# One written list of steps for the change of phases in a graph layer, with the key contexts back to back on TensorE

## The reference, cut to what matters

```python
xn = _layernorm(x)
# graph part: out[dst] += (xn @ weight[rel])[src] * norm
transformed = jnp.einsum('ni,rio->rno', xn, weight)          # 16 types
gnn = segment_sum(transformed[rel_type, src] * norm, dst, num_segments=N)
# mix part: softmax of the keys over the nodes, context of each head, gate
k = softmax(k, axis=1); context = einsum('bnhd,bnhv->bhdv', k, v)
mix = einsum('bnhd,bhdv->bnhv', q, context) * sigmoid(gelu(...) @ Wg2 + bg2) @ Wproj + bproj
x = x + gnn + mix
# experts on the layer norm of the new x, top 2 of 8
tokens = _layernorm(x); out = tokens
for e in range(8):
    out = out + combine[:, e:e+1] * (gelu(tokens @ w1[e] + b1[e]) @ w2[e] + b2[e])
x = x + out
```

## Time and profile before

| | us |
|---|---|
| median of 3 runs | 1601.22 |
| lowest and highest run | 1599.69, 1601.41 |
| span of the profiled execution | 1685.8 |
| its TensorE busy, share of the span | 1601.8, 95% |

### The profile page before, as it was taken

One profiled execution on the slowest core, in us unless ns is written; L12 is line 12 of the kernel. 1 busy time (PEld: TensorE's weight loads), 2 busy tenths in 40 slices (PEclk: granted clock), 3 DMA queues, 4 the chain that ended last, 5 costly groups with the idle time before them and its releaser, 6 DMA issues.

```text
span 1685.8 us, 31748 instructions
## 1 busy us (share of the span) xinstructions
PE 1601.8 (95%) x10509; PEld 1451.7 (86%) x10509; DVE 1340.2 (79%) x3389; ACT 961.4 (57%) x2156; POOL 999.6 (59%) x1111
## 2 busy tenths in 40 slices
PE   7999999999999989998789999999999999999998
PEld 6888888777877878786689999999999999999998
DVE  7888565577777777775569999889999999999985
...
GB/s 295 267 258 246 235 226 238 222 242 242 259 249 242 257 228 252 238 265 271 203 98 100 108 104 112 100 102 101 117 101 106 101 116 100 99 109 110 104 62 10
DMA packets 127076, 290.50 MB, mean 172 GB/s; under 512 B 21271, under 2 KB 49724, under 8 KB 126914
## 3 DMA queue, kind: packets, MB, share of 16 engines
...
## 4 chain that ended last, share of the span: by engine, by line
PE 67%; DVE 12%; issue 8%; ACT 6%; another core or an unknown queue 3%; POOL 2%; DMA 1%; SPq 0%; DVEq 0%; ACTq 0%; POOLq 0%
PE bank L1821 52%; PE bank L2025 3%; PE bank L2026 2%; PE bank L1865 2%; PE bank L1866 2%; ACT mh L1030 2%; DVE ml L1606 2%; DVE ml_a L1357 1%; POOL stg L814 1%; PE bank L1977 1%; DVE ht L1722 1%; DVE xres L1736 1%; ACT raw L1086 1%; DVE stg L1224 1%
## 5 line engine op out<-in xcount | busy, mean ns | idle before, releaser
L814 POOL DMA_INDIRECT stg<-table,idxcur x495 | 530.6, 1072 | 263.9 <-issue 172.9
L1821 PE MATMUL bank<-wreg,xt 128*128 128x512 f32 x2352 | 589.9, 401 | 7.3 <-issue 6.5
L1821 PEld LDWEIGHTS bank<-wreg,xt 128*128 128x128 f32 x2352 | 438.6, 191 | 100.5 <-issue 11.4
L696 POOL DMA_INDIRECT raw<-table,idxa x297 | 302.5, 1018 | 147.3 <-issue 85.4
L1821 PE MATMUL bank<-tt,wreg 128*128 128x256 f32 (+1 forms) x2400 | 319.5, 282 | 0.0
L1821 PE MATMUL bank<-wreg,ht 128*128 128x256 f32 x2352 | 314.7, 283 | 0.4 <-DVE ht L1722 0.2
L1821 PEld LDWEIGHTS bank<-tt,wreg 128*128 128x128 f32 x2400 | 296.4, 189 | 2.9
L1821 PEld LDWEIGHTS bank<-wreg,ht 128*128 128x128 f32 x2352 | 293.2, 189 | 0.9 <-DVE ht L1722 0.4
L1086 ACT ACTIVATE raw<-bank,cols 128x256 f32<-128x256 f32 (+1 forms) x400 | 164.4, 462 | 132.7 <-remote 72.6
L1224 DVE COPY stg<-bank 128x512 f32<-128x512 f32 x196 | 134.2, 686 | 110.4 <-PE bank L1821 76.1
L1606 DVE SCALAR_TENSOR_TENSOR ml<-stg,nrm,mh 128x256 fp32r<-128x256 f32 x455 | 195.5, 478 | 13.4 <-ACT mh L1030 12.8
...
## 6 DMA issues: line engine op xcount, KB each, us to landing
...
```

The source lines that it names most:

```text
L696: pool.indirect_dma_start(ring_a[:, r * EARLY + j, :], None, table[0:LIMIT, :], bass.IndirectOffsetOnAxis(ap=idxa[:, at:at + 1], axis=0)). ...
L814: pool.indirect_dma_start(stg[:, (s % 4) * SUP + j, :], None, table, bass.IndirectOffsetOnAxis(ap=idxcur[:, at:at + 1], axis=0)).then_inc( ...
L1821: mm = pe.matmul(dst, stat(a, c), mov(b, c), start=(n == 0), stop=(n == 3 * chunks - 1))
```

## The change

The first twenty-four groups of sums (pairs 0, 1 and 2), pair 0's way through the experts, and pair 1's up to its second expert are no longer taken from slot tables. One list, `CHANGE`, names their steps in order; `follow` runs it on every engine, which takes the entries that it has a step for. The slot table takes over at pair 3. `SLOTS_OF_SECOND`, `PARTS_OF_SLOT`, `SPLITS` and the lines that hung steps on slots go. In detail:

- On TensorE the held rows and all six parts of the returned rows stand back to back, and pair 0's first sums behind them. The contexts' further steps stand between pair 0's sums.
- The shifts and exponentials of parts 0 and 1 stand ahead of the end of phase one on VectorE and ScalarE. SP issues the loads of the first five rows behind the second table store of the last tile, the other two of `slot` when the kept contexts are done.
- Pair 0's experts begin behind group 3 of pair 1, not behind group 7, with the sums of pair 1 and of pair 2 between them.
- The splits of expert weights are in halves of a chunk, eight on each engine, spread over the list.
- Whole f32 messages are used for the first 20 groups, not the first 16.
- `hf` and the small tiles of the expert choice move out of `raw`, to `ctxbd` with `dg`, to `wv`, and to a new tile `mix`.
- The activation table for Gelu is loaded in pair 0's sums. `roots2` for pair 0 goes ahead of the second gather of group 4 of pair 1 (now: the first of group 5), for pair 1 ahead of group 5 of pair 2 (now: the second of group 7).

```diff
-    ROOTS, FIRST_ROOTS = (7, 1), (5, 0)
+    ROOTS, EARLIER_ROOTS = (7, 1), {1: (4, 1), 2: (5, 0)}
+    FREE_ROWS = 5
...
-        hf = [rs[:, 2048 + 512 * b:2560 + 512 * b] for b in range(2)]
+        hf = [cd[:], wv[:].rearrange("p c n -> p (c n)")]
...
+                    if at(k, NT - 1) and h == 1:
+                        sp.wait_ge(sum_a, ER)
+                        for b2 in range(2):
+                            sp.wait_ge(kv_st[b2], 16 * ((KEPT + SLOTS) // 2))
+                        for n in range(FREE_ROWS):
+                            load_row(n // 4, n)
...
-            load_rows(0)
-            load_rows(1)
+            sp.wait_ge(ctx1_mm, KEPT)
+            for n in range(FREE_ROWS, SLOTS):
+                load_row(1, n)
             first_phase_over(sp)
...
+            def SPLIT(n, h):
+                act.wait_ge(raw_in[n % 2], 32 * (n // 2 - 1))
+                if n >= 6:
                     act.wait_ge(ctx_mm, HELD + REST)
+                act.copy(wreg[:, HI, place_of(n), h * CC // 2].rearrange("p r o -> p (r o)"),
+                         raw[:, n % 2, h * WC * C:(h + 1) * WC * C]).then_inc(w_hi, 1)
...
-WHOLE = 2
+WHOLE_GROUPS = 20
...
+CHANGE = (
+    "HELD_ROWS", "ROWS_OF 0", "FADE", "SELECT 0 0", "SELECT 0 1", "ROWS_OF 1", "SHIFT 2", "EXP 2", "ROWS_OF 2", "SHIFT 3",
+    "EXP 3", "ROWS_OF 3", "MSGS 0 0", "SHIFT 4", "EXP 4", "ROWS_OF 4", "MSGS 0 1", "SHIFT 5", "EXP 5", "ROWS_OF 5", "MSGS 0 2",
+    "GELU_TABLE", "MSGS 0 3", "SPLIT 4 0",
+    "CONTEXT", "SUMS 0 0", "CONTEXT_PE", "SUMS 0 1", "SELECT 0 2", "CONTEXT_TURN", "VALUES", "SUMS 0 2", "ADDS 0 0",
+    "SELECT 0 3", "HEADS", "QUERY", "SUMS 0 3", "CLEAR", "SELECT 0 4", "MSGS 0 4", "QUERY_ROWS", "GATES 0 2", "GATE_ACT 0 2",
+    "SUMS 0 4", "OUT 0 2", "ADDS 0 1", "SPLIT 4 1", "SELECT 0 5", "GATE 0 2", "GATE_HI 0 2", "MSGS 0 5", "SUMS 0 5",
+    "GATE_LOW 0 2", "PROJ 0 2", "ADDS 0 2", "SELECT 0 6", "MSGS 0 6", "SUMS 0 6", "SPLIT 5 0", "SELECT 0 7", "MSGS 0 7",
+    "SUMS 0 7", "SPLIT 5 1", "SELECT 1 0", "MSGS 1 0", "SUMS 1 0", "ADDS 0 3", "SELECT 1 1", "MSGS 1 1", "SUMS 1 1", "ADDS 1 0",
+    "STATS 0 2", "SELECT 1 2", "MSGS 1 2", "SUMS 1 2", "SPLIT 6 0", "MEAN 0 2", "NORM 0 2", "SPLIT 6 1", "TURN 0 2",
+    "TURN_HI 0 2", "TURN_LOW 0 2", "MSGS 1 3", "SELECT 1 3", "LAYER1 0 2 0", "LOGIT 0 2", "SUMS 1 3", "LAYER1 0 2 1",
+    "TOP 0 2", "LOW 0 2 0", "ADDS 1 1",
+    "WEIGHT 0 2", "SELECT 1 4", "LOW 0 2 1", "SPLIT 7 0", "COMB 0 2", "COMB_HI 0 2", "MSGS 1 4", "LAYER1 0 2 2",
+    "LAYER2 0 2 0", "OUT 1 2", "SUMS 1 4", "GATES 1 2",
+    "COMB_LOW 0 2", "SELECT 1 5", "ADD 0 2 0", "LOW 0 2 2", "GATE_ACT 1 2", "GATE 1 2", "LAYER1 0 2 3", "LAYER2 0 2 1",
+    "GATE_HI 1 2", "MSGS 1 5", "SUMS 1 5", "SPLIT 7 1",
+    "ADD 0 2 1", "SELECT 1 6", "LOW 0 2 3", "GATE_LOW 1 2", "ADDS 1 2", "LAYER1 0 2 4", "LAYER2 0 2 2", "MSGS 1 6",
+    "SUMS 1 6", "COMBT 0 2",
+    "ADD 0 2 2", "SELECT 1 7", "LOW 0 2 4", "COMBT_ACT 0 2", "LAYER1 0 2 5", "PROJ 1 2", "LAYER2 0 2 3", "MSGS 1 7",
+    "SUMS 1 7",
+    "ADD 0 2 3", "SELECT 2 0", "LOW 0 2 5", "ADDS 1 3", "LAYER1 0 2 6", "MSGS 2 0", "LAYER2 0 2 4", "SUMS 2 0",
+    "SELECT 2 1", "MSGS 2 1", "SUMS 2 1",
+    "ADD 0 2 4", "LOW 0 2 6", "ADDS 2 0", "STATS 1 2", "SELECT 2 2", "LAYER1 0 2 7", "MSGS 2 2", "LAYER2 0 2 5", "SUMS 2 2",
+    "BIAS2 0 2", "SELECT 2 3",
+    "ADD 0 2 5", "MEAN 1 2", "NORM 1 2", "LOW 0 2 7", "BIAS2_ADD 0 2", "MSGS 2 3", "LAYER2 0 2 6", "SUMS 2 3", "TURN 1 2",
+    "TURN_HI 1 2", "TURN_LOW 1 2", "ADDS 2 1", "SELECT 2 4", "MSGS 2 4", "SUMS 2 4", "SELECT 2 5",
+    "ADD 0 2 6", "LAYER1 1 2 0", "LOGIT 1 2", "MSGS 2 5", "LAYER2 0 2 7", "LOW 1 2 0", "SUMS 2 5", "LAYER1 1 2 1", "TOP 1 2",
+    "ADD 0 2 7", "ADDS 2 2", "SELECT 2 6", "MSGS 2 6", "SUMS 2 6", "SELECT 2 7", "MSGS 2 7", "SUMS 2 7",
 )
+def follow(order, **steps):
+    for entry in order:
+        name, *numbers = entry.split()
+        if name in steps:
+            steps[name](*map(int, numbers), *((8,) if name in OF_GROUPS else ()))
...
-    for i in range(2, pairs):
+    for i in range(3, pairs):
```

More of the change, by code:

```diff
@@ L1010, in _ @@
             held_exps()
+            for ready in range(2):
+                EXP(ready)
             first_phase_over(act)
@@ L1022, in MSGS @@
                 at = EB * (4 * i + s // 2) + EARLY + (s % 2) * CUT
-                if isinstance(i, int) and i < WHOLE:
+                if whole(S):
                     for j in range(n):
@@ L1093, in slot_of @@
             def slot_of(i, s, groups, p1, n1, p2, n2):
-                if s == 0 and not isinstance(i, int):
-                    act.activation(small[0:1, 156:157], small[0:1, 157:158], ACT.Gelu).then_inc(table_kept, 1)
-                if isinstance(i, int) and i + s == 0:
-                    beside(i, s)
                 in_slot(i, s, groups, p1, n1, p2, n2, MSGS=MSGS, GATE_ACT=GATE_ACT, GATE_HI=GATE_HI, NORM=NORM,
                         TURN_HI=TURN_HI, WEIGHT=WEIGHT, COMB_HI=COMB_HI, COMBT_ACT=COMBT_ACT, LAYER1=LAYER1)
-                if isinstance(i, int) and (i, s) == (0, 7):
-                    query_high()
-                    GATE_ACT(0, 2)
-                if isinstance(i, int) and i + s > 0:
-                    beside(i, s)
+            follow(CHANGE, EXP=EXP, SPLIT=SPLIT, GELU_TABLE=GELU_TABLE, QUERY_ROWS=QUERY_ROWS, MSGS=MSGS,
+                   GATE_ACT=GATE_ACT, GATE_HI=GATE_HI, NORM=NORM, TURN_HI=TURN_HI, WEIGHT=WEIGHT, COMB_HI=COMB_HI,
+                   COMBT_ACT=COMBT_ACT, LAYER1=LAYER1)
             run(slot_of, NP, TAIL_GROUPS)
@@ L1598, in MSGS @@
                     return
-                if isinstance(i, int) and i < WHOLE:
+                S = 8 * i + s
+                if whole(S):
                     return
                 at = EB * (4 * i + s // 2) + EARLY + (s % 2) * CUT
-                done = (EB - EARLY) * (4 * i + s // 2) + (s % 2) * CUT
+                done = tiles_before(S)
                 for j in range(PART[s % 2]):
@@ L1766, in slot_of @@
             def slot_of(i, s, groups, p1, n1, p2, n2):
-                if isinstance(i, int) and i + s == 0:
-                    for part in PARTS_OF_SLOT[0]:
-                        shifts(part)
-                    fade_kept()
                 in_slot(i, s, groups, p1, n1, p2, n2, SELECT=SELECT, MSGS=MSGS, WINDOW=WINDOW, LAST_WINDOW=LAST_WINDOW, GATE=GATE,
@@ L1970, in held_contexts, with ROWS_OF @@
                     mm.then_inc(ctx_mm, 1)
-            def contexts(part):
+            def ROWS_OF(part):
                 rows = rows_of(part)
@@ L2151, in _ @@
             pe.wait_ge(add_a, ALL_ADDS)
+            follow(CHANGE, HELD_ROWS=HELD_ROWS, ROWS_OF=ROWS_OF, CONTEXT_PE=CONTEXT_PE, VALUES=VALUES, QUERY=QUERY,
+                   SUMS=SUMS, OUT=OUT, GATES=GATES, PROJ=PROJ, TURN=TURN, LOGIT=LOGIT, COMBT=COMBT, BIAS2=BIAS2,
+                   LAYER1=LAYER1, LAYER2=LAYER2)
             run(slot_of, NP, TAIL_GROUPS)
@@ L2181 @@
 )
-SLOTS_OF_SECOND = (
-    ("*SELECT", "*MSGS", "*WINDOW", "+GATE", "+GATE_HI", "+GATE_LOW", "*SUMS"),
-    ("*SELECT", "*MSGS", "+PROJ", "*SUMS"),
-    ("*SELECT", "*MSGS", "*WINDOW", "+STATS", "*SUMS"),
-    ("*SELECT", "*MSGS", "+MEAN", "+NORM", "*SUMS"),
-    ("*SELECT", "*WINDOW", "+TURN", "+TURN_HI", "*MSGS", "+TURN_LOW", "*SUMS"),
-    ("*SELECT", "+LAYER1 0", "+LOGIT", "*MSGS", "*LAST_WINDOW", "+LOW 0", "*SUMS"),
-    ("*SELECT", "+TOP", "*MSGS", "*WINDOW", "+LAYER1 1", "*SUMS"),
-    ("*SELECT", "*MSGS", "*SUMS"),
-)
+OF_GROUPS = ("SELECT", "MSGS", "SUMS", "ADDS")
+CHANGE = (
[27 rows of a table added]
+)
+def follow(order, **steps):
[3 more added lines that the diff above has]
+            steps[name](*map(int, numbers), *((8,) if name in OF_GROUPS else ()))
 def in_slot(i, s, groups, p1, n1, p2, n2, **steps):
-    for entry in (SLOTS_OF_SECOND if isinstance(i, int) and i == 1 else SLOTS_OF_PAIR)[s]:
+    for entry in SLOTS_OF_PAIR[s]:
         name, *expert = entry[1:].split()
```

170 lines of the change are left out of this document (71 added, 99 removed).

## The result

| | us |
|---|---|
| kernel before, median | 1601.32 |
| changed kernel, median (lowest, highest) | 1628.08 (1624.30, 1631.67) |
| ratio, with its 95% interval | 1.0161 [1.0137, 1.0185] |
| span of the profiled execution after | 1624.0 |

The change costs 26.8 us, by the medians of four runs of each kernel. The forecast was 10.9 us (1612, with 1622 as the upper end): the sign was right, the size was not.

The account below looks back on a forecast made before the run. TensorE, busy 95% of the span, was taken as the bound. Milestone: start 839.3 + work 44.8 + waits 15.3 + clock 2.8 = 902.2 against 891.3, 10.9 us later; 1601.2 + 10.9 = 1612 us, range 1597 to 1622.

Parts of the forecast that it names:

- Part 1: Returned rows: five early loads let TensorE start at 783.9, waits 0.7 us (0 to 4), rows end 803.3, not 812.7.
- Part 2: Pair 0's sums behind the rows: roots behind 21 gathers, then the chain; `LAYER1 0 2 0` at 839.3, now 842.6.
- The rival of the splits: Ahead of pair 0's roots: five half splits each hold up a gather 1.17 us, experts 5.3 later, 1617; chance 10%.
- Part 4: Sums of pairs 1 and 2 wait for messages because of the list's order: 15.8 us, net 15.3, bounds 10 and 20.
- Part 5: TensorE's clock from `LAYER1 0 2 0`: first two twelves of matmuls at half speed, 2.8 us more, between 0 and 6.
- part 3: TensorE's work from `LAYER1 0 2 0` to pair 1's third expert: 44.8 us, milestone 884.1 before waits, a credit of 7.2.
- The rival by which each of nine waits costs the clock: Second stretch: a twelve at half speed after each wait, 1.41 us each, 12.7 in all, time 1625; chance 9%.
- 2 us for the start: Allowance for the start in the range's high end of 1622, beside waits of 20 and clock of 6.
- part 2's own upper bound: Start of `LAYER1 0 2 0` at 844.6 if every half split holds up a gather, against 839.3 taken.

Follow-up runs that it names:

- e7_norows: Changed kernel without the early loads: all 21 returned rows issued behind the kept contexts; 1631.2 us, ratio to before 1.0182.
- e4_load: Changed kernel with the last weight chunk and pair 1's inputs loaded only when group 1 1 has been summed; 1622.0 us, ratio to before 1.0118.
- e2_msgs: Changed kernel with messages of groups 1 4 to 2 7 scaled ahead of the expert steps, TensorE's order untouched; 1615.5 us, ratio to before 1.0086.
- e10_list: Changed kernel, list further reordered: messages ahead of experts, splits as wanted, pair 0's later groups ahead of its gate, late loads behind group 1 1; 1604.9 us.
- e9_before: The kernel before, unchanged, traced a second time; span 1605.3 us, milestone 109.6 us after the first held row.
- e8_nolow: Changed kernel with VectorE's half splits of chunks 4 and 5 cut to 16 columns of 1024; 1623.8 us, ratio to before 1.0128.
- e1_sums: Changed kernel with pair 0's first four sums again between the last four lots of returned rows; 1625.3 us, ratio to before 1.0146.
- e6_best: Changed kernel with messages ahead of experts, first sums between and behind rows, chunk 6's splits behind the chain, last chunk and pair 1's inputs later; 1608.1 us.

## Why the forecast had the sign and not the size

**Part 1, right but small.** The rows begin at 3.5, as said (4.2). All lots waited 3.4 us together, not 0.7, within its bounds; the rows end at 25.6 and not at 23.6. `e7_norows` prices the early loads at 4.4 us for the rows, and at 3.1 by the medians for the whole, which its runs do not set apart from the scatter.

**Part 2, the step that failed.** "The roots for pair 0 come behind 21 gathers" took GpSimd for the pace and a gather's landing for nothing. The 21st gather started 56.2 us after the first held row (forecast 51.2): 2.0 from the rows, 0.9 from the signal that frees the ring, 2.1 from the gathers themselves (five took 1.19 to 1.99 us, 2.6 beyond the 0.5 that was costed for VectorE's splits; index copies took 0.4 less). But then the roots waited 4.08 us more, for group 1 1, `ADDS 1 0` and `STATS`, and ran 0.8 longer beside a split: they ended at 63.2 and not at 53.4. `e4_load` shows the cause: the last of the weight chunks, which the prediction let "keep their places behind the rows and move up with them", and pair 1's inputs behind it were issued into the landing of group 1 1, which took 6.7 us for 3.0. What followed the roots was 1.0 shorter than forecast. `LAYER1 0 2 0`: 68.4, forecast 59.6, the largest part of the miss, 8.8 us.

The rival of the splits was right on the mechanism: of the five half splits three held up a gather and one the roots. Its price was too high at 1.17 each: these three took 0.55 to 1.04 us longer, about what was left of the subtraction. The Trainium skill, "SBUF — State Buffer", section SBUF: two separate sides, says that of a GpSimd instruction that reads SBUF and a VectorE one with two SBUF inputs whichever starts first has the shared port pair to its end, and the other is blocked. The trace agrees for a gather behind a subtraction: one that started 0.05 us behind the split at 755.80 took 1.99 us. It does not show the other direction: a gather that started at 731.68, 0.26 us ahead of a subtraction, took 0.94, but that subtraction took 0.96 us, as the same one at 738.74 did with no gather beside it. And in `e2_msgs` gathers 0.03 and 0.01 us behind a split (757.07, 766.82) took 0.95. The 3.27 of the earlier trace rows can be read so too: that gather started at 817.47 beside an addition (816.84, 0.88 us), which the split of 2.27 us followed at 817.64. The 1.08 there, which started 0.01 us behind a split, fits no better than those two, and stays open.

**Part 4, right.** The waits were put at 15.8 and are 14.5. All but those of groups 2 6 and 2 7 (2.9 together for 3.4) lie within 0.2 us of their forecast: the single ones 1.26 to 1.27 for 1.4, `SUMS 2 4` 2.74 for 2.6. `e2_msgs` confirms the cause: with the messages ahead 10.7 us of the second stretch go.

**Part 5, mis-sized.** TensorE's 51.05 busy us in the second stretch are 6.7 over part 3's work (44.8 less the 0.5 of idle time in it), where the clock had 2.8, bound 6. The start took some 3.5 of that, worked out from rows (the first `LAYER1` 2.59 for 1.41, the second 2.06, the logits 1.5 for 0.8, `SUMS 1 3` 1.9 for 0.9); most of the rest, some 2.1, lies behind groups 2 4 and 2 6, whose waits the prediction had forecast without their clock. The rival by which each of nine waits costs the clock falls: from 803 to 835 it stays at 1.00 through five. That its 1625 comes nearest to the measured 1628 is luck. The Trainium skill, "TensorE: Matmul & The Clock Gate", section HAM oscillation, says that gaps in each round of a loop can bring the clock down again and again: the trace of the changed kernel agrees for the waits of 2.6 and 2.7 us, not for those of 1.3. Nor does the length of a wait settle it: in `e2_msgs` waits of 2.25 and 2.64 us (ahead of 808.85 and 839.60) left the clock up, and in `e10_list` one of 1.93 (ahead of 857.88) did not:

```profile
808.85:815.00 6.15, 6.15 (x46) 5.91 (x47) 3.78 (x9) 2.09 (x6) 2.86 (x3) 1.00 0.28 50
839.60:845.00 5.40, 5.40 (x45) 5.37 (x46) 4.25 (x17) 1.92 (x6) 4.18 (x5) 1.00 0.39 107
```

```profile
857.88:861.90 4.02, 4.02 (x22) 4.02 (x23) 2.74 (x7) 3.39 (x8) 3.14 (x3) 0.60 0.32 86
```

What decides it stays open.

**The sum.** 10.9 forecast; 8.8 more in part 2; 2.65 more in the second stretch (3.9 of clock less 1.3 of waits); 2.0 because the trace had a milestone of 111.6 and `e9_before` has 109.6; 1.4 behind the milestone: 25.8. What is left of the 26.8, 1.0 us (1.8 if the 0.8 that the end wins back is taken off), is not explained and below what the runs scatter. The range ended at 1622 because it took 2 us for the start, where part 2's own upper bound, 844.6, lay 5.3 above the value taken; and even that bound held nothing for the landing.

Which group lands late follows, in the four traces looked at, from where the last chunk falls among the gathers: it is the first group whose last gather is issued behind the chunk's first load. In the changed kernel and `e8_nolow` that is group 1 1 (767.62 behind 766.53, 765.04 behind 764.18). In `e1_sums` and `e2_msgs` the last gather of group 1 1 goes out ahead of the chunk (764.41 and 766.23, 766.82 and 768.10), and group 1 2 is the late one.

Not settled: how much of the changed kernel's scatter (1624 to 1632) this place makes; whether the chunk or pair 1's inputs hold up the gather, since `e4_load` moves both; and the 2 to 3 us by which `e6_best` and `e10_list` are slower than `TURN` of pair 2 says.
